# Mean and variance of the last stage's LayerNorm moved to ScalarE, one batch further ahead

## What is computed

```python
def _layernorm(x, axis=-1, eps=1e-05):
    m = jnp.mean(x, axis=axis, keepdims=True)
    v = jnp.var(x, axis=axis, keepdims=True)
    return (x - m) / jnp.sqrt(v + eps)

def block_quant(v, m_bits, bk):          # bk = 32, m_bits = 3
    amax = jnp.max(jnp.abs(vb), axis=-1, keepdims=True)
    e = jnp.floor(jnp.log2(jnp.maximum(amax, tiny)))
    scale = jnp.exp2(e - m_bits)
    return jnp.round(vb / scale) * scale

def _L1_ffn_ref(x, w_fc, b_fc, w_proj, b_proj):      # w_fc 1024x256, w_proj 256x1024
    h = lowprec_linear(x, w_fc, b_fc, M_BITS_FC, BLOCK_K)
    h = jax.nn.gelu(h, approximate=False)
    return lowprec_linear(h, w_proj, b_proj, M_BITS_PROJ, BLOCK_K)

x = x + jnp.tanh(g_ffn[1]) * _L1_ffn_ref(_layernorm(x, axis=-1), ...)
```

## Time and profile before

| | |
|---|---|
| median of 3 runs | 809.97 us (808.48 to 810.51) |
| the profiled execution | 810.57 us, span 808.5 us |
| busy in the span: PE / DVE / ACT / POOL | 691.2 / 694.7 / 483.2 / 432.8 us |
| mean granted TensorE clock | 0.953 |
| last stage, from about | 648 us |

### The profile page before, as it was taken

The page is one execution under the profiler, slowest core; times in us unless marked ns, Lnnn a source line. Parts: engine busy times, 40 slices in busy tenths (PEclk is TensorE's granted clock), DMA queues, the critical chain, the costliest instruction groups (busy, mean ns, idle before and its releaser), DMA issues.

```text
span 808.5 us, 16554 instructions
## 1 busy us (share of the span) xinstructions
PE 691.2 (85%) x5075; PEld 503.9 (62%) x5090; DVE 694.7 (86%) x1237; ACT 483.2 (60%) x948; POOL 432.8 (54%) x331
## 2 busy tenths in 40 slices
PE   2376999999999998789999999999999766776786
PEld 1265888888888886565665566666565433454454
DVE  6995888888888777968999999998998688999995
ACT  3344555455454442428888887888888556556653
POOL 3643665656655555744444554555443535666553
PEclk9788999999999999889999999999999799889998
DMA  8710000000000000010000000000001000100011
GB/s 271 235 54 0 2 1 1 0 0 0 0 0 1 1 1 1 1 39 17 3 2 2 1 1 1 1 1 1 1 1 54 2 1 0 40 26 26 27 40 53
DMA packets 17719, 18.35 MB, mean 23 GB/s; under 512 B 1670, under 2 KB 16912, under 8 KB 17680
## 3 DMA queue, kind: packets, MB, share of 16 engines
q1 hardware_dynamic: 17084, 17.66, 6.8%
q10 hardware_dynamic: 596, 0.20, 0.1%
HBM read 13.39 MB, written 4.19 MB: 22 GB/s over the span
## 4 chain that ended last, share of the span: by engine, by line
PE 50%; DVE 26%; issue 11%; ACT 5%; DMA 3%; POOL 2%; DVEq 1%; SPq 1%; POOLq 0%; ACTq 0%
PE ps_o L558 9%; PE a_ps_t L599 7%; DVE maxima L1579 5%; PE a_ps_pv L657 5%; PE ps_gu L522 4%; PE ps_gu L524 4%; PE ps_gu L523 4%; DVE f_hcode L1687 4%; DVE f_ps_small L1671 4%; PE a_ps_s L642 3%; PE a_ps_m L619 3%; DMA ctx<-in_ctx 2%; PE a_ps_t L619 2%; PE a_ps_pv L665 2%; ACT stack_t L966 1%
## 5 line engine op out<-in xcount | busy, mean ns | idle before, releaser
L1579 DVE TENSOR_REDUCE maxima<-a_ps_m 128x2 f32<-128x512 f32 x176 | 116.1, 681 | 16.8 <-PE a_ps_t L619 11.3
L975 ACT ACTIVATE probs<-a_ps_s 128x512 f32<-128x512 f32 x196 | 115.7, 601 | 24.3 <-PE a_ps_s L642 19.6
L558 PE MATMUL ps_o<-w2t,hqt 128*128 128x256 f32 (+1 forms) x384 | 99.1, 392 | 1.2 <-ACT hqt L893 0.7
L1202 POOL TENSOR_TENSOR stack<-roped,stack 128x512 f32<-128x512 f32 x32 | 42.7, 1333 | 106.0 <-DVE stack L1569 104.6
L522 PE MATMUL ps_gu<-w1h,yth 128*128 128x352 f32 x256 | 88.4, 345 | 9.6 <-DVE h L1375 6.3
L966 ACT CAST stack_t<-a_ps_t 128x512 fp32r<-128x512 f32 x128 | 71.7, 585 | 32.1 <-PE a_ps_t L599 32.1
L619 PE MATMUL a_ps_m<-stack_t 64*128 64x256 f32 x352 | 80.9, 327 | 10.2 <-DVE maxima L1579 8.8
L657 PE MATMUL a_ps_pv<-probs,v_aug 128*32 128x256 f32 x1024 | 83.6, 399 | 3.5 <-ACT probs L975 3.5
L523 PE MATMUL ps_gu<-w1l,yth 128*128 128x352 f32 x256 | 85.0, 332 | 0.0
L524 PE MATMUL ps_gu<-w1h,ytl 128*128 128x352 f32 x256 | 84.8, 331 | 0.0
L599 PE MATMUL a_ps_t<-idf,stack 128*128 128x128 f32 x512 | 77.0, 292 | 8.9 <-POOL stack L1202 5.1
(11 more groups left out here) (186 smaller groups left out, 1761.4 us busy)
## 6 DMA issues: line engine op xcount, KB each, us to landing
xres<-in_x SPq DMA_DIRECT2D x16, 256.0 KB, 3.2
ctx<-in_ctx SPq DMA_DIRECT2D x16, 256.0 KB, 3.9
out_x<-f_y SPq DMA_DIRECT2D x16, 256.0 KB, 2.1
w1a_raw<-in_w_gate_up SPq DMA_DIRECT2D x1, 1024.0 KB, 6.2
w_raw<-in_w_fc SPq DMA_DIRECT2D x1, 1024.0 KB, 5.6
w_raw<-in_w_proj SPq DMA_DIRECT2D x1, 1024.0 KB, 4.9
w_raw<-in_w_down SPq DMA_DIRECT2D x1, 704.0 KB, 9.7
stack_t<-neg_max_t SPq DMA_DIRECT2D x32, 8.0 KB
```

The costliest lines, as they stand in the source:

```text
L558: ins = nc.tensor.matmul(ps_o[:, c, :], hqt[0:rows, g, n, :], w2t[0:rows, k, :], start=k == 0, stop=k == KH0 - 1)
L975: nc.scalar.activation(a_probs[:, u % 8], score_bank(b, u), ACT.Exp).then_inc(a_exp, 1)
L1579: nc.vector.tensor_reduce(a_maxima[:, b.par, c, 4 * quad + half:4 * quad + half + 3:2], max_bank(m), X, ALU.max).then_inc(a_v_max, 1)
```

## The change

DVE keeps the statistics of batches 0 to 5. From batch 6 on ACT takes them, at the end of its body of batch b for batch b+7: an Identity pass with scale -1/(16 D) whose accumulator output is minus the mean over 16, and a Square pass of x/16 with that as its bias, whose accumulator output is the variance. Each pass also writes its elements to a tile that nobody reads. GpSimd adds epsilon (`f_eps`, `f_var_eps`) and takes the power, in its body of batch b for batch b+7 in place of b+6; in body 0 it takes that of batch 6 first. DVE's `f_shift` reads the new mean. `FFN_AHEAD` goes from 6 to 7, so one pair of batches more is straight code on each engine.

```diff
--- before.py
+++ after.py
...
@@ -135,7 +136,8 @@
 NQ = (I1 + D) // P
 L0_AHEAD = 4
 L0_BEHIND = 4
-FFN_AHEAD = 6
+FFN_AHEAD = 7
+ON_VECTOR = 6
 FFN_BEHIND = 2
 TG = 8
 MU = 16
...
@@ -263,6 +265,9 @@
         f_xt = high("f_xt", [P, 2, KD, C, P], BF16)
         f_y = high("f_y", [P, 2, C, D], F32)
         f_hmag = high("f_hmag", [P, 2, F_NBH], F32)
+        f_var_eps = high("f_var_eps", [P, 2, C], F32)
+        f_mean = high("f_neg_mean_16th", [P, 2, C], F32)
+        f_unused = high("f_unused", [P, 2, 2 * C, D], BF16)
         keep.enter_context(lasting)
         keep.enter_context(left)
         keep.enter_context(right)
@@ -365,6 +370,7 @@
         f_stored = [sem("even_rows_stored"), sem("odd_rows_stored")]
         f_stores_begun = sem("stores_begun")
         f_alone = sem("f_waits_alone")
+        f_a_stats, f_g_var = sem("f_a_stats"), sem("f_g_var")
         def f_blocks(t):
             return t.rearrange("p (q e) -> p q e", e=QB1)
         def f_spread(t, n):
@@ -1018,6 +1024,7 @@
                 act.wait_ge(f_v_shift, b.count(1, 1))
                 if b.shifted(-2):
                     act.wait_ge(f_g_up, b.shifted(-2).count(1, 1))
+                act.sem_inc(f_alone, 1)
                 for c in range(C):
                     nc.scalar.activation(f_xn[:, b.par, c * D:(c + 1) * D], tiles(xres, b)[:, c, :], ACT.Identity,
                                          bias=f_shift[:, b.par, c:c + 1], scale=f_rstd[:, b.par, c:c + 1]).then_inc(f_a_norm, 1)
@@ -1039,6 +1046,22 @@
                 if b.shifted(-2):
                     act.wait_ge(f_t_o, b.shifted(-2).count(C, c + 1))
                 nc.scalar.copy(f_ht[:, b.par, c].rearrange("p k t -> p (k t)"), f_ps_h[c][:, :].bitcast(BF16)).then_inc(f_a_h, 1)
+
+            def ff_input_stats(b):
+
+                done = b.shifted(-ON_VECTOR).count(2 * C, 0)
+                act.wait_ge(f_g_rstd, b.shifted(-2).count(1, 1))
+                act.wait_ge(f_v_shift, b.shifted(-2).count(1, 1))
+                act.sem_inc(f_alone, 1)
+                for c in range(C):
+                    nc.scalar.activation(f_unused[:, b.par, c], tiles(xres, b)[:, c, :], ACT.Identity, scale=-1.0 / (16 * D),
+                                         accum_out=f_mean[:, b.par, c:c + 1]).then_inc(f_a_stats, 1)
+                for c in range(C):
+                    act.wait_ge(f_a_stats, done + c + 1)
+                    act.sem_inc(f_alone, 1)
+                    nc.scalar.activation(f_unused[:, b.par, C + c], tiles(xres, b)[:, c, :], ACT.Square, scale=1.0 / 16,
+                                         bias=f_mean[:, b.par, c:c + 1],
+                                         accum_out=f_var[:, b.par, c:c + 1]).then_inc(f_a_stats, 1)
 
             def ff_body(b):
                 fwd = b.shifted(2)
@@ -1054,6 +1077,8 @@
                 if b.shifted(3):
                     ff_input_out(b.shifted(3))
                 ff_hidden_out(b, 1)
+                if b.shifted(7):
+                    ff_input_stats(b.shifted(7))
 
             act.dma_start(idf[:, :], ident).then_inc(const_loaded, 16)
             act.dma_start(dec[:, :, :], decay).then_inc(const_loaded, 16)
@@ -1099,6 +1124,7 @@
                 ff_gelu(lead[1], u)
             ff_input_out(lead[2])
             ff_norm(lead[4])
+            ff_input_stats(lead[6])
             over_batches(act, ff_body, FFN_AHEAD, FFN_BEHIND)
 
         @block.gpsimd
@@ -1232,10 +1258,17 @@
                     w34_round(1)
 
             def ff_input_rstd(b):
-                pool.wait_ge(f_v_ln, upto(V_LN1, b, "var"))
+                var = f_var[:, b.par]
+                if b.shifted(-ON_VECTOR):
+                    pool.wait_ge(f_a_stats, b.shifted(-ON_VECTOR).count(2 * C, 2 * C))
+                    nc.gpsimd.tensor_tensor(f_var_eps[:, b.par], var, f_eps[:, :], ALU.add).then_inc(f_g_var, 1)
+                    pool.wait_ge(f_g_var, b.shifted(-ON_VECTOR).count(1, 1))
+                    var = f_var_eps[:, b.par]
+                else:
+                    pool.wait_ge(f_v_ln, upto(V_LN1, b, "var"))
                 if b.shifted(-2):
                     pool.wait_ge(f_a_norm, b.shifted(-2).count(C, C))
-                nc.gpsimd.tensor_tensor(f_rstd[:, b.par], f_var[:, b.par], neg_half[:, :], ALU.pow).then_inc(f_g_rstd, 1)
+                nc.gpsimd.tensor_tensor(f_rstd[:, b.par], var, neg_half[:, :], ALU.pow).then_inc(f_g_rstd, 1)
 
             def ff_input_up(b):
                 pool.wait_ge(f_v_in, upto(V_IN1, b, "magic"))
@@ -1255,9 +1288,12 @@
                 if b.shifted(3):
                     ff_input_up(b.shifted(3))
                 ff_hidden_up(b)
-                if b.shifted(6):
-                    ff_input_rstd(b.shifted(6))
-
+                if not b.shifted(-1):
+                    ff_input_rstd(lead[6])
+                if b.shifted(7):
+                    ff_input_rstd(b.shifted(7))
+
+            nc.gpsimd.memset(f_eps[:, :], EPS)
             nc.gpsimd.memset(neg_half[:, :], -0.5).then_inc(g_laid, 1)
             nc.gpsimd.memset(eps[:, :, :], EPS).then_inc(g_const, 1)
             nc.gpsimd.memset(minus_one[:, :, :], -1.0).then_inc(g_const, 1)
@@ -1633,7 +1669,8 @@
                 dve.wait_ge(f_g_rstd, b.count(1, 1))
                 if b.shifted(-2):
                     dve.wait_ge(f_a_norm, b.shifted(-2).count(C, C))
-                nc.vector.scalar_tensor_tensor(f_shift[:, b.par], f_mv[:, b.par, :, 0], -1.0, f_rstd[:, b.par],
+                mean, unit = (f_mean[:, b.par], 16.0) if b.shifted(-ON_VECTOR) else (f_mv[:, b.par, :, 0], -1.0)
+                nc.vector.scalar_tensor_tensor(f_shift[:, b.par], mean, unit, f_rstd[:, b.par],
                                                ALU.mult, ALU.mult).then_inc(f_v_shift, 1)
 
             def ff_norm(b):
@@ -1701,8 +1738,6 @@
                     ff_input_shift(b.shifted(5))
                 if b.shifted(1):
                     ff_hidden_magic(b.shifted(1))
-                if b.shifted(6):
-                    ff_input_stats(b.shifted(6))
                 if b.shifted(3):
                     ff_input_codes(b.shifted(3))
                 for c in range(C):
```

More of the change, by code:

```diff
@@ L100, in build @@
         neg_half = sb("neg_half", [P, C], F32)
+        f_eps = sb("f_eps", [P, C], F32)
         loaded = [keep.enter_context(nc.semaphore(name)) for name in ("even_rows_loaded", "odd_rows_loaded")]
@@ L116, in build @@
         build_main(nc, load, loaded, out_v, g_xattn, g_ffn, w_gate_up, w_down, w_fc, b_fc, w_proj, b_proj, ident, decay,
-                   rope_cos, rope_sin, alibi, xres, ctx, gates, idf, idb, neg_half,
+                   rope_cos, rope_sin, alibi, xres, ctx, gates, idf, idb, neg_half, f_eps,
                    w1h, w1l, w2t, dec, w_fc_t, w_proj_t, bias3, ones3, tiles, weights.close)
```

## The result

The changed kernel takes 852.51 us (851.57 to 853.83), the kernel before 810.16; the ratio is 1.0527, with a 95% interval from 1.0506 to 1.0549. The forecast was 866.5 with a range from 853 to 884, so 56.5 us more; measured are 42.4 more. The sign and the mechanism held, the size did not, and the time lies 0.5 under the range. The profiled execution has a span of 850.7 us and a run time of 852.67.

A forecast was written before the change was run, and what follows sets the result against it. The prediction took a serial loop through GpSimd's f_hup and ACT's whole body to bound the changed last stage: 49.9 us for eight turns plus 6.6 on the way in, 56.5 more, makes 866.5 us; range 853 to 884.

The forecast's parts named there:

- The new loop: Last stage: f_hup, ACT's whole body, four passes, GpSimd's two operations, f_xup, next f_hup; a turn of 15.27 us, now 9.03.
- The first rival: Last stage: faster, only DVE's relief counts, as the passes fit into ACT's pause; -3.1 us, 806.9; chance 0.04.
- GpSimd's pair: GpSimd's add and pow after ACT's statistics, 1.07 us to the next start; high end 1.40.
- The four passes: ACT's two Identity and two Square passes with accumulator outputs, at the end of its body: 2.78 us a turn.
- the low end: Smallest case: passes 1.96 us (4 x 0.49), body 6.10, pair 1.07, turn 13.88; 853 us for the kernel.
- eight turns: Bodies 1 to 8 of the last stage, each 6.24 us longer, 49.9 us more together.
- the way in: Passes for batch 6 and body 0, up to the end of batch 1's f_hup: 6.6 us later.
- ScalarE's body: ACT's body from the end of f_hup to the end of its last copy: 6.67 us a turn.
- DVE's relief: Statistics taken off DVE in ten batches: at most 3.1 us, nearer 9 if f_xcode were not held; not subtracted.
- GpSimd's wait: In the changed stage, GpSimd's largest wait is f_var_eps for ACT's Square, some 6 us each.
- No table load: Rival: Square is not in Gelu's table, so loads join the loop; 13 to 26 us more, 880 to 893; chance 0.07.
- DVE at 60%: Sign in the changed kernel's last stage: DVE falls to about 60% busy.

The follow-up runs named there:

- e1_rstd_six: Changed kernel, but GpSimd's body b takes the power of batch b+6 in place of b+7; 805.75 us.
- e2_stats_first: Changed kernel, but ScalarE takes the statistics of b+7 at the start of body b, ahead of the GELU; 805.95 us.
- e4_passes_twice: Changed kernel plus four more Identity passes with accumulator output per batch ahead of ScalarE's four, results unused; 871.10 us.
- e8_ahead_seven: Kernel before with FFN_AHEAD 7 alone; 809.18 us.
- e3_no_stats: Kernel before with the statistics of batches 6 to 15 left out, GpSimd taking the power of older buffer contents; 805.97 us.
- e11_no_stats_psum: e3_no_stats plus a PSUM copy of the input magnitudes, which f_xcode reads; 803.94 us.
- e9_psum_shift: e6_six_psum with DVE's f_shift taken in body b for b+6, right behind the two f_hcode; 804.82 us.
- e6_six_psum: e1_rstd_six plus a PSUM copy of the input magnitudes, written by one more DVE instruction and read by f_xcode; 807.98 us.

## Why the prediction was wrong in size and right in mechanism

- *The new loop.* As forecast: nine turns lengthened, 8.65 again from batch 9 on. Its proof is e1_rstd_six and e2_stats_first. The first rival needed GpSimd's pair to be over 4.1 us after `f_hup`; it was over after 9.6 (725.18 to 734.79), where 10.6 had been worked out.
- *The four passes, the term that was mis-sized.* 2.78 us predicted, 1.78 measured, and even the low end of 1.96 was above it. I had priced each pass like `f_xn` (0.60 long, 0.49 from one to the next), which has two pointer operands, where the Identity has none and the Square one; the trace had a nearer row, the Square of 512 columns in 0.639. And I had added each read-out at its full 0.205; it takes 0.19, starts 0.10 before its pass ends and lets the next pass start 0.09 after it, so Identity and read-out advance the engine by 0.40, Square and read-out by 0.49. By the working's own structure 1.0 us less makes 8.0 us in eight turns and 2.0 on the way in: 856.5 in place of 866.5, inside the range. The low end with 1.78 would have been about 851.
- *The Trainium skill's figures* (ScalarE: Activation LUTs, section What ACT_TABLE_LOAD costs) had given 2.2 us and a sum 6 us lower. The trace agrees with the passes themselves: 0.40 to 0.42 for an Identity, 0.49 to 0.50 for a Square with its pointer, where the page's formula makes 0.40 and 0.49.
- *What is left.* The spans grew by 42.2 us: -3.3 up to the end of the first `f_hup`, +4.0 on the way in (14.15 against 10.19), +41.3 in eight turns (113.61 against 72.27), +0.2 behind them. The -3.3 had no term. In thirteen profiles the first `f_hup` starts anywhere in 4.4 us, and the changed kernel's profiled execution is the earliest. e4_passes_twice, with the same code up to there but for four passes, starts it 1.9 later. Only 0.7 of the 3.3 are there when ScalarE loads GELU's table (653.98 against 654.67). The rest comes from there to the first `f_hup`, a stretch of 10.8 to 13.7 us in the thirteen profiles: 13.5 before, 10.8 after, 11.6 in e8_ahead_seven, 13.5 in e3_no_stats. I take it for scatter between executions, but each kernel has one profile, so no run here settles it; the range should have had 2 us for it.
- *ScalarE's body and the clock.* 6.67 predicted and measured; the mean granted clock in the stage fell from about 0.90 to 0.73, while PE's busy share fell from 74 to 62% (668 to 754 us before, 700 to 804 us after). No run here holds the one fixed and changes the other.
- *DVE's relief.* 3.1 forecast, 3.4 measured without statistics. It went under in the changed kernel, as forecast. The 9 us that it would be worth without the hold were tested too: e11_no_stats_psum has an F 8.7 lower than the kernel before, a time 5.9 lower.
- *GpSimd's wait* was to be some 6 us each and is 8.5. The prediction's own terms give 6.67 + 2.78 + 0.10 = 9.55 from the end of `f_hup`, so the 6 did not follow from them.
- *No table load* stands between Square and GELU: that rival is out.
- *DVE at 60%* was wrong: 77%, since the held `f_xcode` counts as busy.

## What to carry to other kernels

When work moves to an engine with idle time, ask at which point of that engine's body it ends and who waits for it in order, not how long the idle time is. Being a batch further ahead helps nothing if producer and consumer both stand at the end of the same body; one body between them is what makes slack. Then look whether a moved tile changes the memory that other instructions read: an `f_shift` of two columns cost 3.4 us once its mean lay in SBUF.

## What was not expected of the hardware

- The hold between DVE and GpSimd asks for no size. A DVE instruction on two SBUF tiles of two columns took 3.56 us (0.15 or 0.16 in e9_psum_shift) when it began 0.10 us after GpSimd's `f_hup`. One input in PSUM makes it go away: `f_xcode` took 0.69 us in all sixteen batches of e6_six_psum; in e1_rstd_six twelve of them took 1.35 to 2.42.
- It works in the other direction as well: GpSimd's add on two columns took 1.26 us (0.20 in most other batches of that run) when it began 0.02 us after DVE's `f_hcode`.
- A profile counts the held time as busy: 4.11 us of DVE for an `f_xcode` that takes 0.69 alone.
- An accumulator output is a second instruction of 0.19 us, and the next pass starts 0.09 us after it does (732.06 and 732.15).
